# Position matmuls of a disentangled attention as two row tiles of 64 rows, one PSUM bank each

## The reference, cut to what matters

```python
scores = q @ k.T / sqrt(8 * 3)
c2p = take_along_axis(q @ pos_k.T, clip(rel + 32, 0, 63))      # rel = log_bucket(s - k)
p2c = take_along_axis(k @ pos_q.T, clip(-rel + 32, 0, 63))
scores = scores + c2p / sqrt(16) + p2c.T / sqrt(16)
ctx = softmax(scores) @ v                                      # then @ Wo + bo
```

## Time and profile before

| | |
|---|---|
| time, median of 3 runs (lowest to highest) | 1432.5 us (1430.92 to 1435.93) |
| the profiled execution: its own time, its span | 1437.29 us, 1435.5 us |
| busy, share of the span | PE 78%, PEld 69%, DVE 67%, ACT 48%, POOL 39% |
| busiest groups of PE | L1159 (two kinds) 198.8 and 190.2 us, L1168 158.1, L1186 155.0 |
| the attention's steps | from 461.5 to about 1213 us of the span |
| mean granted clock of TensorE | 0.886 of 2.4 GHz |

### The profile page before, as it was taken

One profiled execution on the slowest core, in us unless ns is written; L12 is line 12 of the kernel. 1 busy time (PEld: TensorE's weight loads), 2 busy tenths in 40 slices (PEclk: granted clock), 3 DMA queues, 4 the chain that ended last, 5 costly groups with the idle time before them and its releaser, 6 DMA issues. The chain is left out here.

```text
span 1435.5 us, 31248 instructions
## 1 busy us (share of the span) xinstructions
PE 1114.9 (78%) x9281; PEld 992.6 (69%) x9281; DVE 966.4 (67%) x2968; ACT 696.1 (48%) x1448; POOL 553.5 (39%) x418
## 2 busy tenths in 40 slices
PE   4990512885626899999999999999999998730886
PEld 3980411784416889888888888888888886630786
DVE  6887731665654777777777777777777776630564
ACT  2434400443533566666666666666666664210443
POOL 0007135553002544444444444454544443026454
PEclk9995555998768999999999999999999999655999
DMA  5910042223289447464646464646565640043221
GB/s 138 206 37 0 1 178 90 76 80 92 71 289 222 103 112 165 111 163 113 164 109 165 112 162 112 162 118 156 125 148 126 147 110 1 1 159 107 63 79 50
DMA packets 75273, 165.91 MB, mean 116 GB/s; under 512 B 8249, under 2 KB 54784, under 8 KB 66528
## 3 DMA queue, kind: packets, MB, share of 16 engines
q1 hardware_dynamic: 69600, 152.75, 42.3%
q0 software_dynamic: 5632, 12.67, 2.6%
HBM read 130.76 MB, written 35.67 MB: 116 GB/s over the span
## 5 line engine op out<-in xcount | busy, mean ns | idle before, releaser
L1131 POOL TENSOR_SCALAR ds_scores<-ds_scores,ds_max 128x256 f32<-128x256 f32 x256 | 348.1, 1360 | 396.7 <-DVE ds_max L1323 396.5
L1315 DVE TENSOR_TENSOR ds_p2c<-ds_bank,ds_p2c 128x512 f32<-128x512 f32 x256 | 175.9, 687 | 95.7 <-PE ds_bank L1168 95.7
L1264 ACT ACTIVATE all_xt<-ds_bank 128x512 f32<-128x512 f32 x256 | 152.9, 597 | 150.1 <-PE ds_bank L1186 150.1
L1159 PE MATMUL ds_bank<-ds_qr,ds_tab 128*128 128x128 f32 x1536 | 190.2, 278 | 21.2 <-DVE ds_qr L1299 18.9
L1159 PE MATMUL ds_bank<-ds_kr,ds_tab 128*128 128x128 f32 x1536 | 198.8, 276 | 0.6 <-ACT ds_p2c L1248 0.6
L1159 PEld LDWEIGHTS ds_bank<-ds_qr,ds_tab 128*128 128x128 f32 x1536 | 182.0, 195 | 23.2 <-issue 23.0
L1248 ACT ACTIVATE ds_c2p_t<-ds_bank 128x512 f32<-128x512 f32 x256 | 152.7, 596 | 92.4 <-PE ds_bank L1159 91.3
L1323 DVE CUSTOM_DVE_ANT_0 ds_scores<-ds_bank,ds_p2c 128x256 f32<-128x256 f32 x512 | 195.3, 418 | 0.3 <-DVE ds_p2c L1315 0.2
L1159 PEld LDWEIGHTS ds_bank<-ds_kr,ds_tab 128*128 128x128 f32 x1536 | 185.2, 193 | 1.0 <-issue 0.8
L1248 ACT ACTIVATE ds_p2c<-ds_bank 128x512 f32<-128x512 f32 x256 | 149.3, 597 | 54.4 <-PE ds_bank L1159 54.3
L1168 PE MATMUL ds_bank<-all_constants,ds_c2p_t 128*128 128x128 f32 x1024 | 158.1, 277 | 0.0
(11 more groups left out here) (244 smaller groups left out, 1746.2 us busy)
## 6 DMA issues: line engine op xcount, KB each, us to landing
ds_qr<-scratch_qk SPq DMA_DIRECT2D x32, 1024.0 KB, 11.0
ds_kr<-scratch_qk SPq DMA_DIRECT2D x32, 1024.0 KB, 13.9
ds_tab<-scratch_tables SPq DMA_DIRECT2D x64, 248.0 KB, 10.6
slots_in<-all_zero SPq DMA_DIRECT2D x2, 5160.0 KB, 42.1
ds_qs<-scratch_q_parts SPq DMA_DIRECT2D x32, 288.0 KB
ds_ks<-scratch_k_parts SPq DMA_DIRECT2D x32, 288.0 KB
0fe_xb<-slots_in SPq DMA_DIRECT2D x40, 129.0 KB
1fe_xb<-slots_in SPq DMA_DIRECT2D x40, 129.0 KB
```

What stands on the lines that cost most here:

```text
L1131: pool.tensor_scalar(S[b % NS][:, 1, :], S[b % NS][:, 1, :], mx[:, 2 * b + 1:2 * b + 2], None, ALU.subtract).then_inc(s_sub1, 1)
L1159: last = pe.matmul(pb[n % 2][:, a * P:(a + 1) * P], TAB[half][:, kind, c:c + P], mov[:, :].rearrange("p (b g s) -> p g b s", b=HALF, s=16) ...
L1264: act.activation(PT[b], pt2[:, :].rearrange("p (k s) -> p k s", k=2), ACT.Exp).then_inc(s_exp, 1)
L1315: dve.tensor_tensor(z, pt1[b % 2][:, :].rearrange("p (a k) -> p a k", a=2), z, ALU.add).then_inc(s_z, 1)
```

## The change

Each near matmul becomes two, on two row tiles of the array. Rows 0 to 63 (8 shifts) serve 8 of a group's 16 positions, rows 64 to 127 the other 8. Each tile has 64 rows, 128 weight columns and 64 moving columns, and writes a bank of its own (`pb[tile]`). A near fill is now eight groups on both tiles, 16 matmuls (32 records), and fills both banks; a set has 6 near fills and 4 far ones. A fill waits for the copies of all banks that it writes. `QR` and `KR` hold only the 1024 columns that their rows use; they are loaded with two DMAs instead of one. `QT` is stored with the two halves of each group of 16 apart. The middle one of three near fills covers two runs of groups, so its copies are four of 256 columns instead of two of 512. `SHARE` puts one near fill in each of steps 0 to 5 and two far fills in steps 6 and 7.

```diff
-                    act.activation(QT[j][:, g * 512:(g + 1) * 512], bank[n % 4][:, :], ACT.Identity,
+                    act.activation(by_halves(QT[j], g), by_groups(bank[n % 4][:, :]), ACT.Identity,
...
-                    dve.tensor_tensor(rest[n % 3][:, :], QT[j][:, cols], part[j][:, 0, cols], ALU.subtract).then_inc(s_rest, 1)
+                    dve.tensor_tensor(by_groups(rest[n % 3][:, :]), by_halves(QT[j], g), by_groups(part[j][:, 0, cols]), ALU.subtract).then_inc(s_rest, 1)
...
-        QR = [m.sb(f"qr{i}", [P, HT]) for i in range(2)]
+        QR = [m.sb(f"qr{i}", [P, HT // 2]) for i in range(2)]
...
-        FILLS = near[:10] + [far[0], near[10], far[1], near[11], far[2], far[3]]
+        RUNS = (((0, 0, 8),), ((0, 8, 4), (1, 4, 4)), ((1, 8, 8),))
+        FILLS = [("near", kind, runs) for kind in range(2) for runs in RUNS] + \
+                [("far", kind, (0, QUADS - 1)) for kind in range(2)] + [("far", kind, (1, 0)) for kind in range(2)]
+        FILLS = FILLS[:6] + [FILLS[6], FILLS[8], FILLS[7], FILLS[9]]
+        BANKS = [2 if f[0] == "near" else 1 for f in FILLS]
+        FIRST = [sum(BANKS[:n]) for n in range(len(FILLS))]
...
-        SHARE = [2, 2, 2, 1, 2, 2, 2, 3]
+        SHARE = [1, 1, 1, 1, 1, 1, 2, 2]
...
-                    sp.dma_start(R[half][:, :], views["qk"][j][:, rows, cols]).then_inc(s_r[half], 16)
+                    for tile in range(2):
+                        sp.dma_start(R[half][tile * 64:(tile + 1) * 64, :], views["qk"][j][1 - tile][:, rows, cols]).then_inc(s_r[half], 16)
...
-                pe.wait_ge(s_be, f + 1)
+                pe.wait_ge(s_be, f + BANKS[n])
...
-                for a in range(4):
-                    grp = 4 * quad + a
+                groups = [(side, grp) for side, grp0, count in where for grp in range(grp0, grp0 + count)]
+                for a, (side, grp) in enumerate(groups):
                     c = TABLE - SEQ + P * side - 16 * grp
-                    last = pe.matmul(pb[n % 2][:, a * P:(a + 1) * P], TAB[half][:, kind, c:c + P],
-                                     mov[:, :].rearrange("p (b g s) -> p g b s", b=HALF, s=16)[:, grp, :, :],
-                                     start=True, stop=True)
-                last.then_inc(s_bm, 1)
+                    for tile in range(2):
+                        last = pe.matmul(pb[tile][:, a * 64:(a + 1) * 64], TAB[half][tile * 64:(tile + 1) * 64, kind, c:c + P],
+                                         mov[tile * 64:(tile + 1) * 64, :].rearrange("p (b g s) -> p g b s", b=HALF, s=8)[:, grp, :, :],
+                                         start=True, stop=True)
+                        if a == len(groups) - 1:
+                            last.then_inc(s_bm, 1)
...
+                for tile in range(2):
+                    act.wait_ge(s_bm, done + tile + 1)
+                    at = 0
+                    for side, grp, count in where:
+                        dst = to[:, side, :, :].rearrange("p b (g h s) -> p h g b s", h=2, s=8)[:, 1 - tile, grp:grp + count, :, :]
+                        last = act.activation(dst, pb[tile][:, at * 64:(at + count) * 64].rearrange("p (g b s) -> p g b s", g=count, b=HALF), ACT.Copy)
+                        at += count
+                    last.then_inc(s_be, 1)
...
-                rows = R[half][:, :].rearrange("p (n s) -> p n s", s=16)
-                dve.tensor_tensor(rows, rows, con["own_pos"].unsqueeze(1).to_broadcast([P, HT // 16, 16]), ALU.mult).then_inc(s_masked, 1)
+                rows = R[half][:, :].rearrange("p (n s) -> p n s", s=8)
+                dve.tensor_tensor(rows, rows, con["own_pos"].unsqueeze(1).to_broadcast([P, HT // 16, 8]), ALU.mult).then_inc(s_masked, 1)
```

More of the change, by code:

```diff
@@ L810, in project_qkv, with by_halves, by_groups @@
         scale = (1.0 / np.sqrt(3.0 * DB), 1.0)
+        def by_halves(tile, g):
+            return tile[:, :].rearrange("p (h n s) -> p n h s", h=2, s=8)[:, g * 32:(g + 1) * 32, :, :]
+        def by_groups(part):
+            return part.rearrange("p (n h s) -> p n h s", h=2, s=8)
         G = TOKENS // 512
@@ L998, in stacked_views @@
         "tables": [bass.AP(tensor=tab, offset=j * P * OFFS, ap=[[1, 16], [OFFS, P], [1, TABLE]]) for j in range(2)],
-        "qk": [bass.AP(tensor=qk, offset=j * P * n, ap=[[0, 16], [n, P], [1, n]]) for j in range(2)],
+        "qk": [[bass.AP(tensor=qk, offset=j * P * n + h * n // 2, ap=[[0, 8], [n, P], [1, n // 2]]) for h in range(2)] for j in range(2)],
         "q_parts": bass.AP(tensor=dram["q_parts"].tensor, offset=0, ap=[[n, rows], [0, 3], [1, n]]),
@@ L1019, in attend @@
         HT = HALF * SEQ
-        QR = [m.sb(f"qr{i}", [P, HT]) for i in range(2)]
-        KR = [m.sb(f"kr{i}", [P, HT]) for i in range(2)]
+        QR = [m.sb(f"qr{i}", [P, HT // 2]) for i in range(2)]
+        KR = [m.sb(f"kr{i}", [P, HT // 2]) for i in range(2)]
         QS = [m.sb(f"qs{i}", [9 * DB, HT], BF16) for i in range(2)]
@@ L1046, in attend @@
         assert (bucket(np.arange(SEQ // 4 + 1, SEQ)) >= BUCKETS - 1).all() and (bucket(-np.arange(SEQ // 4 + 1, SEQ)) <= -BUCKETS).all()
[L1047 to L1050, removed]
-        FILLS = near[:10] + [far[0], near[10], far[1], near[11], far[2], far[3]]
-        CONTENT_FILLS = 1 + max(n for n, f in enumerate(FILLS) if f[0] == 0)
+        RUNS = (((0, 0, 8),), ((0, 8, 4), (1, 4, 4)), ((1, 8, 8),))
[4 more added lines that the diff above has]
+        FIRST = [sum(BANKS[:n]) for n in range(len(FILLS))]
+        BM = sum(BANKS)
+        CONTENT_FILLS = FIRST[8]
         views = stacked_views(dram)
         LAG = 3
-        SHARE = [2, 2, 2, 1, 2, 2, 2, 3]
+        SHARE = [1, 1, 1, 1, 1, 1, 2, 2]
         block = stack.enter_context(nc.Block())
@@ L1140, in fill @@
             def fill(head, half, n):
-                kind, quad, side = FILLS[n]
-                f = (2 * head + half) * BM + n
+                what, kind, where = FILLS[n]
+                f = (2 * head + half) * BM + FIRST[n]
                 if n == 0:
@@ L1147, in fill @@
                 pe.wait_ge(s_masked, 2 * (2 * head + half) + kind + 1)
-                pe.wait_ge(s_be, f + 1)
+                pe.wait_ge(s_be, f + BANKS[n])
                 mov = (QR, KR)[kind][half]
-                if is_far(quad, side):
+                if what == "far":
+                    side, quad = where
                     pe.wait_ge(s_stack[half], 16 * 4 * (head + 1))
-                    pe.matmul(pb[n % 2][:, :], ENDS[half][:, kind, side * FAR:(side + 1) * FAR],
+                    pe.matmul(pb[FIRST[n] % 2][:, :], ENDS[half][:, kind, side * FAR:(side + 1) * FAR],
                               (QS, KS)[kind][half][:, :].rearrange("p (b s) -> p b s", b=HALF)[:, :, quad * 64:(quad + 1) * 64],
@@ L1228, in _ @@
             pe.sem_inc(s_av, 2)
-            for n in range(BM):
+            for n in range(len(FILLS)):
                 fill(0, 0, n)
@@ L1240, in copy @@
             def copy(head, half, n):
[L1241 to L1248, removed]
+                what, kind, where = FILLS[n]
+                done = (2 * head + half) * BM + FIRST[n]
+                to = (CT, PC)[kind][half]
+                if what == "far":
+                    side, quad = where
+                    act.wait_ge(s_bm, done + 1)
+                    act.activation(to[:, side, :, quad * 64:(quad + 1) * 64], pb[FIRST[n] % 2][:, :].rearrange("p (b s) -> p b s", b=HALF),
+                                   ACT.Copy).then_inc(s_be, 1)
+                    return
+                for tile in range(2):
[6 more added lines that the diff above has]
+                    last.then_inc(s_be, 1)
             def head_values(head, half):
@@ L1448, in shape_constants @@
         "head_of": row[:, None] // DA == np.arange(HA)[None, :],
[L1450 removed]
+        "own_pos": 7 - row[:, None] // DB % 8 == np.arange(8)[None, :],
         "iota_b": np.broadcast_to(np.arange(BLOCKS), (P, BLOCKS)),
```

9 lines of the change are left out of this document (5 added, 4 removed).

## The result

The changed kernel took 1492.1 us, median of 4 runs (1491.07 to 1493.79), against 1434.2 us for the kernel before, measured beside it (1430.92 to 1437.8): ratio 1.0407, 95% interval 1.0384 to 1.043. It is slower by 58 us. The forecast was 1489 us, in a range from 1425 to 1650. The executions of each kernel in this document lie within 0.8% of each other, except one of the four of run a5 (2624.8 us), which is left out of its time and ratio.

The account below looks back on a forecast made before the run. PE's stream was taken to bound the attention. 31 sets x (0 near matmuls + 1.52 tile mode + 0.30 net waits) = 56.4 us more: 1493.7 us for the profiled execution, median 1489, range 1425 to 1650.

Parts of the forecast that it names:

- PE bounds the attention, and masks and DMAs taken off gain nothing: In the attention, PE's stream sets the pace, so smaller masks and halved loads on other engines gain 0.
- The near matmuls: In near fills, a pair of tiles keeps one record's pitch, 0.1117 us, bound by weight loads: no change, 0.
- The rival with half the time: In near fills, a row tile's load costs half or is hidden: pair pitch 0.058 us, 1335 us; chance 0.12.
- Change of tile mode: Around near fills, six entries at 0.17 us and five exits at 0.10 add 1.52 us per set.
- The waits for both banks: Before near fills, PE waits for all copies of the last fill: 0.75 us more per set.
- the far fill's wait: In far fills, the wait for ACT's copy goes, as two banks are free: 0.45 us less per set.
- The first set: Before the first transposes, earlier loads and mask against longer near fills: taken as 0, bounds -3 and +3.
- the direction: For the whole kernel, the change makes it slower: chance 0.83.
- No change, with modes that cost nothing: For the whole kernel, modes cost nothing and ACT's chain is hidden better: 1432 us; chance 0.05.
- Instruction supply as the bound: In PE's stream, supply of 312 record pairs per set instead of 216 limits: 1489 to about 1760 us; chance 0.08.
- Loads one after the other: In near fills, the two tiles' loads do not overlap: 10.7 us per set more, 1821 us; chance 0.05.
- A load that does not go under its own matmul: In near fills, row mode bares the tile's load: 5.1 us per set more, 1647 us; chance 0.08.

Follow-up runs that it names:

- a5: The changed kernel, but in the first set alone one weight load serves two groups (128 moving columns per tile instead of 64): 1483.2 us, ratio 1.0334.
- a1: The changed kernel, but in all sets after the first each row tile streams 32 moving columns instead of 64, loads kept: 1493.1 us, ratio 1.0397.
- a2: The changed kernel, but one weight load serves two groups: 4 matmuls of 128 moving columns per tile and fill instead of 8 of 64: 1311.4 us, ratio 0.9131.
- a3: The changed kernel, but both matmuls of a pair use rows 0 to 63, so one row tile: 2439.0 us, ratio 1.6984.
- b2: The kernel before with the changed kernel's fill order and wait for both banks, but matmuls of 128 rows and no row tiles: 1426.6 us, ratio 0.9915.
- b1: The kernel before, but every near matmul contracts only rows 0 to 63, with the same records, columns, order and waits: 1526.1 us, ratio 1.062.
- c1: The kernel before, but the near matmuls of steps 0, 1 and 2 alone contract only rows 0 to 63: 1465.1 us, ratio 1.0205.
- b3: The kernel before with two fills in every step, instead of 1 in step 3 and 3 in step 7: 1420.3 us, ratio 0.987.
- a4: The changed kernel with the first set's near fills in turn on two pairs of banks, so fills go back to back: 1487.3 us, ratio 1.0351.

## Why the forecast was right, and where it was not

**PE bounds the attention, and masks and DMAs taken off gain nothing.** PE is busy 24.88 of a set's 24.93 us after, while DVE lost 2.1 us and a set got longer. No run takes the smaller masks and loads alone, so this is read from the profile and not shown by an experiment.

**The near matmuls: 0.** The number is shown: the pair's pitch is 0.111 us (forecast 0.1117). a1 and a2 show that the streamed columns do not set it, a3 that the tiles run side by side. That what is left is the load's 128 columns, and not some other price per record on a tile, is argued from the earlier trace rows and from the load's unchanged length. The rival with half the time is excluded by the pitch itself.

**Change of tile mode: 1.52 us per set.** b2 has the change's order and waits, but no row tiles: 23.42 against 24.93, so 1.51 us, near the forecast (the bank waits of the two kernels differ by some 0.1 us, so the last digit means nothing). b1 and c1 price a way in and out at 0.29 to 0.34 with 128 moving columns, where the forecast had 0.27 and `after` itself shows 3.18 us for the step of 813.32 against 2.91 in b2, 0.27.

**The waits for both banks: +0.75, and -0.45 for the far fill, net +0.30.** Here the size was off: b2 shows -0.32 for both together, and b3 -0.65 for the far fill's wait alone, which leaves 0.33 for the waits for both banks. The links of the chain from ACT's start on were too long. In the changed kernel two copies take 1.09 us, not 1.15, four of 256 columns 1.21, not 1.41, and PE starts 0.06 after them, not 0.14 + 0.07; an ordinary fill does not wait at all, and the one after a middle fill 0.12 (810.02 to 813.32 is 3.30, 813.32 to 816.50 is 3.18). Over 31 sets the term was 19 us too high.

**The first set: 0, bounds -3 and +3.** This failed. It costs 13 us up to the first transposes, and 5.5 behind them. I had taken half clock for the first fills alone, as in the kernel before. A first fill takes 3.68 us and 1.3 of waiting, not 1.67 + 1.62. The loads and the mask were to be done 4 us earlier, and the first fill started 1.4 us earlier: half the bytes did not land sooner, as the first mask waited 6.64 us for them, before 6.60:

```profile
434.67 1.23 DVE L1325 TENSOR_TENSOR ds_qr<-ds_qr,all_constants 128x1024 f32<-128x1024 f32 x1 [6.64 <-DMA ds_qr<-scratch_qk]
```

The step was wrong by 18.5 us, outside its bounds, and it hid the 19 us of the step before: the sum came out 3 us from the measured median because two errors cancelled, which is luck. What is confirmed is the direction, the main term and the mode's price, not the 1489.

**Rivals.** No change, with modes that cost nothing: excluded by b1 and c1. Instruction supply as the bound: it needed more than 0.081 us per pair of load and matmul, and inside a fill 32 pairs come every 0.055 us, in `av` sixteen every 0.046. At the half clock the 0.055 become (3.68 - 0.42) / 31 = 0.105 (0.42 us is one record there), so the pace in a fill goes with the array's clock. Loads one after the other: excluded by a3. A load that does not go under its own matmul: excluded by the pitch of 0.111.

**What stays open:** why the clock stays low at the start of the changed kernel. It is not the gaps (a4), nor the first set's fills alone (a5). It rose early with 128 rows (at 441.6 us before, 442.6 in b3, 450.1 in b2), with 64 rows in three steps only (452.7, c1) and with two tiles of 128 columns everywhere (458.3, a2); late with two tiles of 64 or 32 columns (503.5 after, 508.5 in a1, 501.2 in a4, 496.1 in a5) and with one tile of 64 rows (506.1 in b1, 544.5 in a3). In each late run it rose only when the last near fill made in the first set's steps was over and PE did other work: in the changed kernel that fill ended at 500.5, in a4 at 497.8, in a5 at 491.4. a3 shows the same over and over: with `av` at 602.6 and at 636.3 it rises at 602.5 and at 640.1, and in between it falls, after one near fill at the full clock (columns as in the earlier trace rows):

```profile
602.53:609.35 6.82, 6.82 (x66) 5.88 (x66) 1.91 (x7) 2.82 (x6) 1.82 (x2) 1.00 0.36 100
609.35:640.07 30.72, 30.72 (x148) 27.69 (x147) 7.07 (x22) 5.98 (x14) 3.57 (x3) 0.50 0.17 51
```

This fits row-tile fills that hold the clock down. But in the steady sets of the changed kernel and of b1 it stays at 1.00 with such fills in the stream, and no run here isolates what makes the difference.

## What to carry to other kernels

Row tiles halve the rows of a weight load and not its time (196 ns against 193 to 195), so count loads before columns. With 128 weight columns, two tiles side by side gained nothing at 64 moving columns per load (2.00 us against 1.95) and much at 128 (1.16 against 1.95); nothing between was measured. Each way in and out of the row tiles cost 0.27 to 0.34 us here, and three steps of it cost 1.03 us per set where eight cost 2.33; so such work is better collected than spread over the steps, as far as the waits allow it. And look at which step issues one fill more than there are free banks: moving one fill from step 7 to step 3 gave 1.3% for one line.

## What the runs showed of the hardware that I had not expected

TensorE's clock can fall in the middle of gapless work: with one row tile of 64 rows and 64 moving columns its mean over the sets was 0.61 of 2.4 GHz, and a fill went from 3.78 to 7.09 us. With both tiles it held 1.00 in the steady sets, but came up only at about 503 us instead of 441.6. In a4 PE's records leave no gap from 441 to 462 us, at 0.50: a PE that looks busy says nothing of its clock, which has to be read in its own column.

A copy by ACT that follows another costs less than its record: two of 512 columns take 1.09 us where one takes 0.595, and four of 256 take 1.21 where one takes 0.389.
